# The nine passes over the node rows of a graph network, written out tile by tile, with scores in the product

## What is computed

```python
x = x + _L0_gnn_ref(_layernorm(x), src, dst, ...)   # relational graph layer, twice
x = x + _L0_ffn_ref(_layernorm(x)[None], ...)[0]    # 8 dense experts, weights softmax(x @ Wr + br)
x = x + _L1_gnn_ref(_layernorm(x), edge_index, ...) # graph convolution, then attention over edges
x = x + _L1_ffn_ref(_layernorm(x)[None], ...)[0]    # 2 of 8 experts, picked from the mean row
x = x + _L2_gnn_ref(_layernorm(x), ...)             # x @ W_self + mean over edges of maxk(x @ W_neigh, 32)
x = x + _L2_ffn_ref(_layernorm(x)[None], ...)[0]    # 2 of 8 experts for each node
x = x + _L3_gnn_ref(_layernorm(x), ...)             # attention (4 heads), layer norm, relu, attention (1 head)
x = x + _L3_ffn_ref(_layernorm(x)[None], ...)[0]    # one expert on the 1561 largest nodes
```

## Time and profile before

| | us |
|---|---|
| median of three runs | 7711.75 |
| the profiled execution, its own time | 7714.48 |
| its span | 7712.8 |
| the nine passes in it, by their windows | 735.4 |

### The profile page before, as it was taken

One profiled execution on the slowest core, in us unless ns is written; L12 is line 12 of the kernel. 1 busy time (PEld: TensorE's weight loads), 2 busy tenths in 40 slices (PEclk: granted clock), 3 DMA queues, 4 the chain that ended last, 5 costly groups with the idle time before them and its releaser, 6 DMA issues. The chain is left out here.

```text
span 7712.8 us, 81237 instructions
## 1 busy us (share of the span) xinstructions
PE 5320.6 (69%) x21589; PEld 3583.0 (46%) x21589; DVE 4335.9 (56%) x6661; ACT 2284.1 (30%) x3965; POOL 1473.0 (19%) x1601
## 2 busy tenths in 40 slices
PE   0223788877888599898597639639925777666976
PEld 0011344443444366677475418538823333335754
DVE  6100599946999322232684460301138999987857
ACT  0000211122111233222363103212215777754611
POOL 0775166602666000001000000030020000000000
PEclk9655899998999699999798869769967888877978
DMA  0011433354334100033230002145523444432200
GB/s 25 26 38 52 188 100 108 99 168 168 110 100 97 43 8 8 10 96 113 87 112 21 1 13 69 36 151 186 182 67 120 155 156 155 149 92 92 91 12 17
DMA packets 379927, 679.26 MB, mean 88 GB/s; under 512 B 94754, under 2 KB 306907, under 8 KB 372156
## 3 DMA queue, kind: packets, MB, share of 16 engines
q1 hardware_dynamic: 304364, 519.11, 20.5%
q0 software_dynamic: 75344, 157.40, 7.9%
HBM read 503.61 MB, written 172.62 MB: 88 GB/s over the span
## 5 line engine op out<-in xcount | busy, mean ns | idle before, releaser
L598 POOL DMA_INDIRECT sum_rows_in<-rel_table,rel_row x880 | 847.8, 963 | 455.1 <-issue 234.5
L622 DVE TENSOR_SCALAR sum_hot_cell<-x_nodes 128x1500 bf16<-128x1500 f16 (+1 forms) x880 | 892.4, 1014 | 1.0 <-issue 0.9
L676 PE MATMUL ps<-sum_hot_cell,sum_hot_src 128*128 128x500 bf16 x2640 | 766.1, 394 | 165.2 <-issue 84.5
L1504 PE MATMUL ps<-att_ring,acc 125*65 125x500 f32 x1000 | 606.8, 693 | 303.8 <-DVE att_ring L1326 303.5
L545 PE MATMUL ps<-rel_diag,rel_xt 128*128 128x512 f32 x800 | 436.1, 693 | 407.7 <-issue 175.7
L681 PE MATMUL ps<-sum_rows_in,sum_hot 128*128 128x256 f32 x1760 | 592.0, 415 | 65.3 <-issue 63.7
L778 PE MATMUL ps<-aux,sum_wide 125*125 125x256 f32 x2500 | 579.1, 387 | 54.5 <-ACT sum_wide L727 54.5
L1512 PE MATMUL ps<-acc,att_ring 125*125 125x257 f32 x2500 | 561.2, 387 | 73.4 <-DVE att_ring L1326 46.0
L942 POOL COPY aux<-prep_xin 128x256 f32 x75 | 30.1, 415 | 2987.4 <-DVE prep_xin L977 2987.4
L1442 ACT ACTIVATE att_ring<-att_ring,att_src 125x625 f32<-125x625 f32 x750 | 545.4, 804 | 126.3 <-DVE att_ring L1307 126.2
L1307 DVE TENSOR_TENSOR att_ring<-att_ring,att_rows 125x3125 f32<-125x3125 f32 (+1 forms) x162 | 512.4, 3169 | 93.8 <-ACT att_ring L1401 92.6
(11 more groups left out here) (432 smaller groups left out, 7532.4 us busy)
## 6 DMA issues: line engine op xcount, KB each, us to landing
att_cell<-cells SPq DMA_DIRECT2D x150, 781.2 KB, 4.7
att_masks<-masks SPq DMA_DIRECT2D x150, 762.9 KB
rel_table<-rel_stage SPq DMA_DIRECT2D x50, 2048.0 KB
ffn_w<-in_L_ffn_W SPq DMA_DIRECT2D x64, 1024.0 KB, 7.3
sum_cell<-cells SPq DMA_DIRECT2D x250, 156.2 KB, 2.2
masks<-sum_stage POOLq DMA_DIRECT2D x25, 762.9 KB, 11.7
sum_rows_in<-rel_table,rel_row POOLq DMA_INDIRECT x880
cells<-x_nodes SPq DMA_DIRECT2D x5, 2031.2 KB
```

Source lines behind the costliest of these rows:

```text
L598: pool.indirect_dma_start(rows_in[:, b, u, :], None, table, bass.IndirectOffsetOnAxis(rows[:, k:k + 1], 0)).then_inc(gathered[b], 16)
L622: dve.tensor_scalar(hot_cell[:, b, u, :], K.columns[:, :, 0:CW], K.cell[:, k], None, ALU.is_equal).then_inc(s_hot, 1)
L676: pe.matmul(K.ps[:, bass.ds(side * 4 + j, 1), 0:BW].rearrange("p a n -> p (a n)"), hot_src[:, b, u, :], hot_cell[:, b, u, j * BW:(j + 1) * ...
L1504: pe.matmul(K.ps[0:W, side, 0:BAND], node_rows[s][0:NPT, h, :], ring[0:NPT, b % RB, v, 0:BAND], start=s == 0, stop=s == NT - 1).then_inc(s ...
```

## The change

`node_pass` is written anew. All 25 tiles are written out, without loops, and waits are on constants.

- VectorE measures (`measure`) two groups ahead, before it waits for the loads; `invert` takes the reciprocal, `write` makes the rows, `use` is what follows the product of the group before.
- TensorE alternates: product of tile t, transposes of tile t + 3. There are three PSUM banks for turned tiles and five for results, each released by itself. It waits for the loads only before the first product.
- Scores: `weigh_vectors` multiplies the weights by the two attention vectors once, and sums give 2 columns per head that are appended to the weights. The product is 258 or 264 columns wide and carries the scores; ScalarE copies them out. The four operations over PSUM are gone.
- Softmaxes: sums and maxima by group, and one exponential over all 25 tiles at the end.
- Rows of gat1 and gat3 come from two fused operations per tile, and relu moves into ScalarE's copy of the turned tile.
- sage: the first `max` and `match_replace` read PSUM, without the copy; ScalarE copies the own rows out, and GpSimd adds them to `x`.
- `xt_nodes` and `aux` are written directly; GpSimd's copies are gone.

Lines that are only removed and stand in the kernel above are mostly left out here.

```diff
-def node_pass(K, tag, w_names, vectors, pre, pre_steps, norm=None, post=None, post_steps=0, act_post=None,
-              table=None, keep_xt=False, keep_xn=False, batch_post=None, batch_steps=0, gate_cols=0, gates_exp=True,
-              ones_cols=None, early=None):
+def node_pass(K, tag, w_names, vectors, pre, norm=None, post=None, act_post=None, pool_post=None, keep_xt=False,
+              keep_xn=False, gates=None, cols=0, scores=None, relu=False, early=None, ones_cols=None):
     nc = K.nc
-    wide = D * len(w_names) if w_names and not gate_cols else gate_cols
+    heads, src_name, dst_name = scores if scores is not None else (0, None, None)
+    wide = cols if gates is not None else D * len(w_names)
+    full = wide + 2 * heads
+    products = bool(w_names)
+    LAG, XB, YB = 3, 2 * UN, UN
...
-        stats, mv = ph.sb("stats", [P, UN, 6]), ph.sb("mv", [P, UN, 2])
+        stats, mv = ph.sb("stats", [P, NT, 6]), ph.sb("mv", [P, NT, 2])
...
+        def row(t):
+            return K.aux[:, t, :] if keep_xn else xin[:, t % XB, :]
+        def turned(t):
+            return K.xt[:, :, t * P:(t + 1) * P] if keep_xt else xt[:, t % XB, :, :]
+        def ps_t(t):
+            return K.ps[:, t % LAG, 0:D]
+        def ps_y(t):
+            if gates is not None:
+                return K.ps[:, LAG + t // UN, t % UN * cols:(t % UN + 1) * cols]
+            return K.ps[:, LAG + t % YB, 0:full]
...
+            def measure(i):
+                tiles = range(i * UN, (i + 1) * UN)
+                for t in tiles:
+                    dve.bn_stats(stats[:, t, :], norm(t)).then_inc(s_stats, 1)
+                for t in tiles:
+                    dve.wait_ge(s_stats, t + 1)
+                    dve.bn_aggr(mv[:, t, :], stats[:, t, :]).then_inc(s_aggr, 1)
+                dve.wait_ge(s_aggr, (i + 1) * UN)
+                var = mv[:, i * UN:(i + 1) * UN, 1]
+                dve.tensor_scalar(var, var, LN_EPS, None, ALU.add).then_inc(s_var, 1)
+            def invert(i):
+                var = mv[:, i * UN:(i + 1) * UN, 1]
+                dve.wait_ge(s_rstd, i + 1)
+                dve.reciprocal(var, var).then_inc(s_inv, 1)
+                dve.wait_ge(s_inv, i + 1)
+            def write(i):
+                tiles = range(i * UN, (i + 1) * UN)
+                if not keep_xn and i >= 2:
+                    dve.wait_ge(s_tr, (i - 1) * UN)
+                for t, ins in zip(tiles, pre(dve, i, tiles, row, tools)):
+                    ins.then_inc(s_pre, 1)
+            def weigh_vectors():
+                dve.wait_ge(loaded, n_loads)
+                f = D // heads
+                for j, name in enumerate((src_name, dst_name)):
+                    dve.tensor_tensor(prod[:, j, :, :], w_sb[:, :, 0:D], vec[name][:, :].unsqueeze(1).to_broadcast([P, DC, D]),
+                                      ALU.mult).then_inc(s_w, 1)
+                dve.wait_ge(s_w, 2)
+                for j in range(2):
+                    for c in range(DC):
+                        dve.tensor_reduce(w_sb[:, c, D + j * heads:D + (j + 1) * heads],
+                                          prod[:, j, c, :].rearrange("p (h f) -> p h f", h=heads), AX, ALU.add).then_inc(s_w, 1)
+            def use(i):
+                if gates is not None:
+                    dve.wait_ge(s_mm, (i + 1) * UN)
+                    gates.batch(dve, link, i, ps_gates(i), tools)
+                elif has_post:
+                    post(dve, link, i, ps_y, s_mm, s_post, tools)
...
+            if norm is not None:
+                measure(0)
+                measure(1)
+            if scores is not None:
+                weigh_vectors()
...
+            for i in range(NT // UN):
+                    invert(i)
+                write(i)
+                if norm is not None and i + 2 < NT // UN:
+                    measure(i + 2)
+                if i > 0:
+                    use(i - 1)
+            use(NT // UN - 1)
+            if gates is not None:
+                gates.final(dve, link, K.ps[:, LAG:LAG + UN, 0:UN * cols].rearrange("p i (u c) -> p i u c", c=cols), tools)
...
+            for t in range(NT + LAG):
+                if norm is not None and t % UN == 0 and 0 < t // UN < NT // UN - 1:
+                    root(t // UN + 1)
+                if t < NT:
+                    act.wait_ge(s_tr, t + 1)
+                    if products and not keep_xt and t >= XB:
+                        act.wait_ge(s_mm, t - XB + 1)
+                    source = ps_t(t).rearrange("p (c f) -> p c f", c=DC)
+                    if relu:
+                        act.activation(turned(t), source, ACT.Relu).then_inc(s_xt, 1)
+                    else:
+                        act.copy(turned(t), source).then_inc(s_xt, 1)
+                if has_act and t >= LAG:
+                    act.wait_ge(s_mm, t - LAG + 1)
+                    if scores is not None:
+                        act.copy(K.score[:, t - LAG, :].rearrange("p (j h) -> p j h", j=2)[:, :, 0:heads],
+                                 ps_y(t - LAG)[:, D:full].rearrange("p (j h) -> p j h", j=2))
+                    act_post(act, t - LAG, ps_y(t - LAG), tools).then_inc(s_apost, 1)
+            if gates is not None and gates.exp:
+                act.wait_ge(s_sum, 1)
+                act.activation(tools.logits[:, :, 0:cols], tools.logits[:, :, 0:cols], ACT.Exp).then_inc(s_exp, 1)
...
+            def turn(t):
+                pe.wait_ge(s_pre, t + 1)
+                if t >= LAG:
+                    pe.wait_ge(s_xt, t - LAG + 1)
+                for c in range(DC):
+                    mm = pe.transpose(ps_t(t)[:, c * P:(c + 1) * P], row(t)[:, c * P:(c + 1) * P], K.ident[:, :])
+                mm.then_inc(s_tr, 1)
+            for t in range(LAG if products else NT):
+                turn(t)
+            if scores is not None:
+                pe.wait_ge(s_w, 2 + 2 * DC)
+            for t in range(NT if products else 0):
+                pe.wait_ge(s_xt, t + 1)
+                if gates is None and t >= YB:
+                    if has_post:
+                        pe.wait_ge(s_post, t - YB + 1)
+                    if has_act:
+                        pe.wait_ge(s_apost, t - YB + 1)
+                for c in range(DC):
+                    mm = pe.matmul(ps_y(t), turned(t)[:, c, :], w_sb[:, c, :], start=c == 0, stop=c == DC - 1)
+                mm.then_inc(s_mm, 1)
+                if t + LAG < NT:
+                    turn(t + LAG)
...
+    def batch(self, dve, link, i, ps, tools):
+        tiles = slice(i * UN, (i + 1) * UN)
+        logits = tools.logits[:, tiles, :]
+        b = tools.vec[self.bias_name][:, :].unsqueeze(1).to_broadcast([P, UN, 8])
+        link(dve.tensor_tensor(logits, ps, b, ALU.add))
+        link(dve.tensor_reduce(tools.top[:, tiles, 0], logits, AX, ALU.max))
+    def final(self, dve, link, ps, tools):
+        logits, top = tools.logits[:, :, :], tools.top[:, :, 0]
+        wide = [P, NT, 8]
+        dve.tensor_tensor(logits, logits, top.unsqueeze(2).to_broadcast(wide), ALU.subtract).then_inc(tools.s_sum, 1)
+        dve.wait_ge(tools.s_exp, 1)
+        link(dve.tensor_reduce(top, logits, AX, ALU.add))
+        link(dve.reciprocal(top, top))
+        dve.tensor_tensor(self.K.gate[:, :, :], logits, top.unsqueeze(2).to_broadcast(wide), ALU.mult)
...
+        link(dve.tensor_tensor(logits[:, here, :], ps, b, ALU.add))
+        link.all([dve.max(best[:, t % UN, :], logits[:, t, :]) for t in tiles])
+        link(dve.tensor_copy(tools.top[:, here, 0], best[:, :, 0]))
+        link(dve.memset(best[:, :, 2:8], BIG))
+        link.all([dve.match_replace(marked[:, t, :], best[:, t % UN, :], logits[:, t, :], -BIG) for t in tiles])
...
-        def gcn_out(dve, turn, it, xin, tools):
-            tiles, wide = bass.ds(it * UN, UN), [P, UN, D]
-            turn(dve.tensor_tensor(xin, K.acc[:, tiles, 0:D], K.aux[:, tiles, :], ALU.add))
-            turn(dve.tensor_tensor(xin, xin, K.dinv[:, tiles].unsqueeze(2).to_broadcast(wide), ALU.mult))
-            turn(dve.tensor_tensor(xin, xin, tools.vec["L1_gnn_b1"][:, :].unsqueeze(1).to_broadcast(wide), ALU.add))
-            return dve.tensor_scalar(xin, xin, 0.0, None, ALU.max)
+        def gcn_out(dve, i, tiles, row, tools):
+            for t in tiles:
+                dve.tensor_tensor(row(t), K.acc[:, t, 0:D], K.aux[:, t, :], ALU.add).then_inc(tools.s_half, 1)
+            dve.wait_ge(tools.s_half, (i + 1) * UN)
+            return [dve.scalar_tensor_tensor(out=row(t), in0=row(t), scalar=K.dinv[:, t:t + 1], in1=tools.vec["L1_gnn_b1"][:, :],
+                                             op0=ALU.mult, op1=ALU.add) for t in tiles]
...
-        def max_k(dve, turn, it, ps, tools):
-            tiles = bass.ds(it * UN, UN)
-            h, best = tools.work[:, :, :], tools.work2[:, :, 0:8]
-            turn(dve.tensor_copy(h, ps[:, :, 0:D]))
-            for _ in range(MAXK // 8):
-                turn.all([dve.max(best[:, u, :], h[:, u, :]) for u in range(UN)])
```

(39 more changed lines are left out.)

322 lines of the change are left out of this document (98 added, 224 removed).

## The result

The changed kernel takes 7423.35 us, the median of four runs (7411.42 to 7435.71), against 7713.59 for the kernel before (7710.52 to 7715.54). The ratio is 0.9619, with a 95% interval of 0.9607 to 0.9630. A second group of five runs of the same kernel gives 0.9615 (0.9598 to 0.9631), median 7410.97.

A forecast was written before the change was run, and what follows sets the result against it. Engines waiting for each other by turns within nine passes in series were taken as the bound; pass savings of 232.6 us plus 5 for starts, 238 off 7714.5, adjusted to the median, gave 7474 us, range 7445 to 7520.

The forecast's parts named there:

- A prep tile at 1.2 GHz: 4.34/5 + 1.08/2: TensorE's product and transposes per tile in prep0, prep2 and prep3: 0.87 + 0.54 = 1.41 us, 25 tiles 35.3 us.
- VectorE stays below: gcn: VectorE has 34 us, below the 39.3 us pass set by TensorE; 4.4 us saved.
- epsilon and four hand-overs some 0.4: VectorE's `measure` per group: this beside statistics 1.73 and aggregates 0.45, hence 2.6 us.
- reciprocal with its waits 0.45: VectorE's `invert` and `write` per group: this plus five rows 1.70, hence 2.15 us.
- only part of the wait goes: sage: TensorE's group still lies between a group's last search result and the next first `max`; 157.1 against 172.1, saved 15.0 us.
- 11.4 us: sage: TensorE's group between search results and next first `max`, 12.3 with transposes, 14.2 to the last `max`.
- Sage under 145 us: Listed sign that the forecast is wrong; sage's window was forecast at about 157 us.
- After the passes: Attention phases: 50 small products may run at 2.4 GHz, vector work begins earlier in three phases; 5 us, bounds 0 and 8.
- The clock stayed at 0.50 in prep0, prep2 and prep3: Against the rival that the clock rises in prep passes: 17 us less in all, 7457 us; chance 0.10.
- hand-over cost per tile: Rival: alternation costs TensorE 0.2 to 0.4 us for each of 150 tiles, 7504 to 7534 us; chance 0.12.
- The clock did not stay low in gcn and the gat passes: Against the rival of a low clock there: twice the time for 100 tiles, 106 us, 7580 us; chance 0.05.
- The written-out code did not stall: Against the rival that instructions from memory stall the engines: at 1.5 us per tile 7812 us; chance 0.02.

The follow-up runs named there:

- the runs by fives: Changed kernel with TensorE taking products of five tiles, then transposes of the next five, instead of alternating per tile: together 10 us longer, prep0, prep2, prep3 +1.9 each.
- the control: The changed kernel as it is, rerun beside the combined kernel, nothing changed: 0.9615 of the kernel before, median 7410.97 us.

## Why the prediction was wrong

The direction, the mechanisms and the order of the passes held; the time fell out of the range because almost every price was too high, and all in the same direction.

**TensorE's price of a prep tile: 1.41 forecast, 1.18 measured.** The step that failed is "A prep tile at 1.2 GHz: 4.34/5 + 1.08/2", which divides the lengths of runs. 25 tiles in three passes make 17 us of the 57 that were missed in the passes; 11 of them are the tails read as work, 6 the gain of the alternation, which I had not seen (the runs by fives put it at 5.6 for these passes).

**TensorE at 2.4 GHz: 1.18 forecast, 1.08 measured** from start to start in gcn, 2.5 us a pass in gcn, gat1 and gat2. Only a small part of it is the same error: by fives, gcn takes 5.77 us from start to start for five tiles, 1.15 each, so 0.03 a tile is tail and 0.07 the alternation. The three first tiles at 1.2 GHz stood in the sum with 3 us and the lead of gat2 with 10.0; the first row came at 9.6.

**gcn: two bounds close together.** I had TensorE as its bound and wrote that VectorE stays below. In the changed kernel that holds: TensorE does not wait once after its first row, and VectorE waits for it near the end.

```profile
DVE aux L2443 <- PE ps L1007: 4.4, 8, 0.6
```

But a faster start of TensorE gave nothing until VectorE's scaling was moved off as well, and then 2.2 us. The margin that the forecast left between the engines is not there. The scaling on ScalarE without the lifted clock was not tried.

**VectorE's hand-overs.** `measure` was to take 2.6 us and takes 2.18, `invert` and `write` 2.15 and take 1.84; a group of prep1 is 4.02 in place of 4.75. The step that failed is "epsilon and four hand-overs some 0.4", with "reciprocal with its waits 0.45": prices read from the old loop, for code without it. Of the 0.73 a group, 0.17 is again tails (the statistics taken at 1.73 are 1.64 from start to start, the rows taken at 1.70 are 1.62). The form of the waits is 0.30, since prep1's later groups take 4.32 with waits by register. The last 0.26 no run explains. Over all passes the old form of the waits, put back, costs 19 us. In prep1 the tail of the pass went the other way, 1.9 us for the last tile in place of 1.4.

**sage: 15.0 forecast, 29.3 by the same measure.** The mechanism (only part of the wait goes) was right and its sizes were not. The rows of a group in the changed kernel, both engines:

```profile
4374.21 1.41 DVE L2492 SCALAR_TENSOR_TENSOR aux<-sage_work,ps 128x256 f32<-128x256 f32 x4
4374.39 3.75 PE L1007 MATMUL ps<-sage_w,sage_xt 128*128 128x512 f32 x4 [15.43 <-issue]
4375.75 1.70 DVE L1016 TENSOR_SCALAR sage_xin<-x_nodes,sage_mv 128x256 f32<-128x256 f32 x5
4377.37 1.72 DVE L876 BATCH_NORM_STATS2 sage_stats<-x_nodes 128x6 f32<-128x256 f32 x5
4384.07 1.88 PE L1007 MATMUL ps<-sage_w,sage_xt 128*128 128x512 f32 x4
4384.95 0.43 DVE L2485 MAX8 sage_best<-ps 128x8 f32<-128x256 f32 x1 [1.51 <-ACT sage_own L2498]
```

From TensorE's start to the end of the last `max` on this group (4387.3) are 12.9 us, forecast 14.2. The five `match_replace` take 2.1 in place of 2.4, a round 3.87 in place of 4.08, and the waits of 0.6 are gone: 27.2 us a group in place of 29.9. The part on VectorE, 1.5 us a group, is the form of the waits, which the run with registers puts at 7.3 us for the pass. The part on TensorE, 1.3 a group, comes from the term "11.4 us". These are the products of groups 2 and 4; the products of the five groups before are 10.06, 11.37, 10.26, 11.40 and 10.28 us long, and the third is

```profile
4514.59 10.26 PE L970 MATMUL ps<-sage_w,sage_xt 128*128 128x512 f32 x20 [19.18 <-DVE x_nodes L2454]
```

The granted clock makes the difference: from 4484 to 4487, 2.4 us into group 2, it is 0.54, and from 4517 to 4520, as far into group 3, 0.92. In the changed kernel it is 0.81 from 4377 to 4380, 2.6 us into the group shown, and the four later groups all take 3.87 to 3.95 us from the first product's start to the second's. I had taken the longer of two lengths. "Sage under 145 us" stood among the signs that I was wrong, and it came.

**gat3, prep2, prep0.** Here several of these errors meet: gat3's group was forecast at 7.5 us and takes 6.5; its fused operations were right (4.09 us for ten from start to start, 4.2 taken), its `measure` and its waits were not. In prep0 the lead was 5.1 us in place of 6.0.

**After the passes: right by luck.** 5 us were forecast for the attention phases, and 5.1 came in the two profiles, but as 5.3 and 4.2 less in two of them and 4.4 more in the third. In the control's profile the same three phases together are 1.8 us longer than in the kernel before. What was forecast of TensorE did come: its 50 products took 5.82 us in place of 8.03 after gat2 and 7.45 in place of 8.61 after gat1. No run shows that the phases got shorter by it.

**The rivals.** The clock stayed at 0.50 in prep0, prep2 and prep3, as the earlier trace rows said. No hand-over cost per tile appeared: TensorE's first wait in gat2 is its only one. The clock did not stay low in gcn and the gat passes. The written-out code did not stall: 24.95 us of records in 25.9 of gat2, beside the loads of cells and masks, leave no room for it.

**The range.** I bounded the clock, the hand-overs and the starts, but gave the prices per tile and per group, on which 150 tiles and 40 group steps rest, no bounds at all. An error of 0.24 us in one of them was outside everything that the range considered.

## What to carry to other kernels

Take the price of a step in a pipelined engine from start to start of two runs, never from the length of a run divided by its count, and give that price a bound of its own when it is multiplied by a hundred tiles. When two engines work by turns over a set of buffers, look for the last reader of a buffer: moving it off (scores into the product, the row into a copy) gave 110 and 19 us here, while fusing, measuring ahead, cheaper waits and the alternation gave 12, 49, 19 and 10. These were taken back one at a time and need not add up; the single softmax, the search from PSUM and the direct writing of `aux` and `xt_nodes` were not taken back alone. In an alternating order ask what each product stands behind. TensorE at 1.2 GHz with a nearly full busy record deserves a try with a wider product: doing more work took a quarter off the pass.

## What I had not expected of the hardware

- Widening a product from 8 to 128 columns made prep0 shorter, 29.7 us from 38.9, since the clock went from 0.50 to 1.00; lifting the clock alone, with the narrow product kept, did not last.
- At 1.2 GHz a stream of transposes and narrow products takes 0.197 us for each load of weights, with the moves beside the loads; by fives it takes 7% more.
- Phases that no edit touches have two or three lengths from run to run. The attention phase after gat2 took 1075.7 us in one profile of the changed kernel and 1086.3 in another, the sum after sage 310.6 or 314, the attention phase after gat3 366.5 or 371. They may be why the five times of the control spread over 29 us (7396.96 to 7426.33) where its passes repeat within 0.6; only one of the five was profiled. The first window of each of the two profiles of that attention phase:

```profile
5583.50:5783.50 200.00, 117.92 (x468) 63.84 (x468) 177.76 (x110) 126.95 (x189) 0.00 (x0) 0.80 0.42 138
```

```profile
5582.00:5782.00 200.00, 119.48 (x468) 64.16 (x468) 177.54 (x110) 126.74 (x188) 0.00 (x0) 0.79 0.42 137
```

  The same work, TensorE 1.56 us longer at a clock of 0.79 in place of 0.80. What sets which length comes was not tried and stays open.
